# One more turn for the FFN: merged weights of a row made in the following turn, with a new timetable

## The reference, cut to what matters

```
h   = layernorm(x)
q   = (h @ Wq.T + bq) / sqrt(16);  k = ctx @ Wk.T + bk;  v = ctx @ Wv.T + bv      # 16 heads
a   = softmax(q @ k.T, over keys) @ v
y   = x + (a @ Wo.T + bo)
g   = layernorm(y)
out = y + ((g @ W1[r].T + b1[r]) @ W2[r].T + b2[r])      # row r has its own W1 (1024x256), W2 (256x1024)
```

## Time and profile before

| what | us |
|---|---|
| median of three runs | 609.21 (607.52 to 611.81) |
| the profiled execution | 607.91 |
| its span, first to last instruction | 606.1 |
| busy: PE, DVE, ACT, POOL | 563.9, 457.4, 392.5, 273.5 |
| TensorE's granted clock, mean | 0.966 |

### The profile page before, as it was taken

How to read it: one execution, slowest core, us unless ns; L and a number is a source line. 1 busy time by engine, 2 the same in 40 slices (tenths; PEclk the granted TensorE clock), 3 DMA queues, 4 the chain that set the end, 5 groups by cost and what they waited for, 6 DMA issues and landing times.

```text
span 606.1 us, 13508 instructions
## 1 busy us (share of the span) xinstructions
PE 563.9 (93%) x4353; PEld 342.9 (57%) x4353; DVE 457.4 (75%) x841; ACT 392.5 (65%) x703; POOL 273.5 (45%) x319
## 2 busy tenths in 40 slices
PE   7799999999999999999999999999899989898987
PEld 7545546565665656555655656565555646353667
DVE  6897896889678876888778876888778976883024
ACT  4225776777667676767767676777768665766541
POOL 5260466046832496046832487046831193017311
PEclk9957999999999999999999999999999999995999
DMA  6684343565444733464344723465434523420201
GB/s 208 130 221 158 87 112 84 134 194 132 105 115 118 227 85 94 136 185 135 105 99 130 226 76 100 119 184 152 105 90 106 159 49 96 129 84 6 86 0 36
DMA packets 46704, 72.67 MB, mean 120 GB/s; under 512 B 12162, under 2 KB 22730, under 8 KB 46666
## 3 DMA queue, kind: packets, MB, share of 16 engines
q1 hardware_dynamic: 46666, 72.18, 43.0%
HBM read 41.99 MB, written 4.47 MB: 77 GB/s over the span
## 4 chain that ended last, share of the span: by engine, by line
PE 65%; DVE 16%; issue 9%; ACT 5%; POOL 2%; DMA 2%; DVEq 1%; SPq 0%; ACTq 0%; POOLq 0%
PE pv L535 16%; PE st L521 13%; PE nat L510 10%; PE misc L709 9%; PE misc L595 7%; DVE neg_max L1040 5%; PE misc L585 3%; DVE stats L1051 3%; ACT probs L878 2%; DVE lo L1062 2%; ACT normed L926 2%; DVE y L1119 2%; POOL norm_in L1277 1%; PE st L501 1%; DVE normedT_lo L1068 1%
## 5 line engine op out<-in xcount | busy, mean ns | idle before, releaser
L1040 DVE TENSOR_REDUCE neg_max<-nat 128x1 f32<-128x512 f32 x504 | 336.9, 683 | 99.3 <-PE nat L510 94.9
L878 ACT ACTIVATE probs<-st 128x512 f32<-128x512 f32 x502 | 293.1, 599 | 147.3 <-PE st L521 136.0
L521 PE MATMUL st<-qs,ks 64*128 64x512 f32 x502 | 229.0, 472 | 14.9 <-ACT probs L878 14.3
L510 PE MATMUL nat<-ks,qs 63*128 63x512 f32 x504 | 236.0, 488 | 5.1 <-DVE neg_max L1040 2.4
L521 PEld LDWEIGHTS st<-qs,ks 64*128 64x128 f32 x502 | 92.9, 190 | 127.9 <-ACT probs L878 114.8
L535 PE MATMUL pv<-probs,vs 128*32 128x512 f32 x1024 | 140.2, 620 | 1.2 <-ACT probs L878 1.2
L510 PEld LDWEIGHTS nat<-ks,qs 63*128 63x128 f32 x504 | 92.8, 189 | 32.0 <-DVE neg_max L1040 26.7
L709 PE MATMUL misc<-w_in 64*128 64x256 f32 x512 | 70.7, 378 | 8.3 <-DVE y L1128 8.3
L709 PEld LDWEIGHTS misc<-w_in 64*128 64x128 f32 x512 | 51.4, 186 | 16.0 <-issue 11.0
L1298 POOL TENSOR_TENSOR pair_ctx<-pair_ctx,inv_sum 128x512 f32<-128x512 f32 x15 | 19.1, 1271 | 89.0 <-DMA inv_sum<-inv_dram 89.0
L535 PEld LDWEIGHTS pv<-probs,vs 128*32 128x32 f32 x1024 | 20.3, 108 | 37.4 <-issue 27.9
(11 more groups left out here) (204 smaller groups left out, 1005.9 us busy)
## 6 DMA issues: line engine op xcount, KB each, us to landing
ks<-hi SPq DMA_DIRECT2D x64, 128.0 KB, 2.4
qs<-hi SPq DMA_DIRECT2D x64, 128.0 KB, 2.5
w_in<-w SPq DMA_DIRECT2D x16, 512.0 KB
w_in<-w2T SPq DMA_DIRECT2D x16, 512.0 KB
x_in<-x SPq DMA_DIRECT2D x8, 512.0 KB, 3.4
ctx_in<-ctxT SPq DMA_DIRECT2D x8, 512.0 KB, 3.6
ks<-lo SPq DMA_DIRECT2D x32, 128.0 KB, 2.4
qs<-lo SPq DMA_DIRECT2D x32, 128.0 KB, 2.5
```

Of the source, the lines that this page charges most:

```text
L510: mm((nat_of(n) if bank is None else bank)[:, :], qs[own, 2 * g + jj, c * P:(c + 1) * P], ks[own, 2 * g + jj, :], start=True, stop=True).t ...
L521: mm(st_of(u, prep)[:, :], ks[rows(jp), 2 * g + jj, kc * P:(kc + 1) * P], qs[rows(jp), 2 * g + jj, :], start=True, stop=True).then_inc(st_ ...
L878: act.activation(probs[kc % 2][:, j, :], st_of(u, prep)[:, :], ACT.Exp).then_inc(exp_done, 1)
L1040: dve.tensor_reduce(neg_max[:, g % 2, at:at + 1], (nat_of(n) if bank is None else bank)[:, :], AX.X, ALU.max, negate=True).then_inc(max_do ...
```

## The change

- W21 of row b is made in turn b + 1 (units 33 to 47) between the last chain links, its split follows at units 47 to 49, `yT` moves to units 51 and 52, and `z` to units 55 to 64, so its last step lies in unit 0 of the turn after. The output halves are added on VectorE in units 1 and 3 of turn b + 2 (`late` is true where there is a row b - 2).
- Turn 0 makes no W21. Turn 7 makes that of row 6 at units 10 to 15 and that of row 7 at units 51 to 63, with tables of its own.
- The FFN load of row b stands at the end of turn b on SP, the one of row 0 no longer before the turns. `store_out` and `load_y` move into the first third of the next turns, `spread_ln` behind `gather_sums`, and `spread_inverse(b, 0)` behind `stack_quad(b + 1, 1)`.
- POOL makes the b2 parts of row b - 1 first in turn b, then `divide` and `add_bo`; `inverse_root(1)` stands ahead of `x_norm`, `add_b2` behind the stacks of v.
- The tables have new units throughout, and `yT`, `z`, `W21` and `maxT` other banks.

The diff, cut to its core:

```diff
-YT_BANKS = (1, 2)
-Z_BANKS = (1, 2)
-W21_BANKS = (0, 1)
-MAXT_BANKS = (2, 1, 2, 0)
-
-CHAIN_UNITS = tuple((4 * k + 2, 4 * k + 2, 4 * k + 3, 4 * k + 3, 4 * k + 4, 4 * k + 4) for k in range(LINKS + 1))
-YT_UNITS = (38, 38, 38, 38, 39, 39, 39, 39)
-Z_UNITS = (44, 44, 45, 45, 47, 47, 48, 49)
-W21_UNITS = (51, 52, 52, 54, 54, 55, 56, 56, 58, 59, 60, 60, 62, 62, 63, 63)
-LAST_W21_UNITS = (50, 50, 51, 51, 52, 52, 54, 54, 55, 56, 56, 58, 58, 59, 60, 60)
-MAXT_UNITS = ((54, 55), (6, 7), (23, 24), (39, 40))
+YT_BANKS = (0, 2)
+Z_BANKS = (1, 0)
+W21_BANKS = (1, 2)
+MAXT_BANKS = (1, 1, 2, 0)
+
+CHAIN_UNITS = ((3, 3, 3, 3, 3, 5), (7, 7, 7, 7, 7, 8), (10, 10, 11, 11, 12, 12), (14, 15, 15, 15, 15, 16), (18, 18, 19, 19, 19, 20), (22, 22, 22, 23, 24, 24), (27, 27, 27, 27, 27, 27), (31, 31, 31, 31, 31, 32), (33, 33, 33, 34, 35, 36))
+YT_UNITS = (51, 51, 51, 51, 52, 52, 52, 52)
+Z_UNITS = (55, 56, 59, 59, 60, 63, 63, 64)
+W21_UNITS = (33, 35, 36, 38, 38, 38, 39, 39, 42, 42, 43, 44, 45, 46, 47, 47)
+LAST_W21_UNITS = (51, 51, 51, 51, 51, 51, 51, 51, 53, 54, 56, 59, 60, 60, 62, 63)
+EARLY_W21_UNITS = (10, 10, 10, 11, 11, 11, 11, 13, 15, 15, 15, 15, 15, 15, 15, 15)
+LAST_YT_UNITS = (39, 40, 42, 42, 43, 43, 43, 43)
+LAST_Z_UNITS = (48, 48, 48, 48, 48, 48, 48, 48)
+MAXT_UNITS = ((52, 53), (4, 5), (23, 24), (37, 39))
 PV_AT = 1
 
-ODD_AT = (34, 2)
-JOIN_AT = (36, 4)
+ODD_AT = (33, 1)
+JOIN_AT = (43, 5)
 EVEN_AT = (19, 51)
-MASK_AT = (22, 54)
-HI_AT = (9, 13, 17, 21)
-LO_AT = (10, 14, 18, 22)
-W21_HI_AT = 0
-W21_LO_AT = 2
-ATTN_AT = (50, 16)
-NORM_AT = 33
-YT_HI_AT = 40
-YT_LO_AT = 41
-X_SPLIT_AT = 52
-CTX_SPLIT_AT = 44
-STATS_AT = 11
-INVERT_AT = (40, 7)
-MAX_AT = (56, 8, 25, 41)
-Y_AT = (25, 29)
-V_AT = (33, 37)
-OUT_AT = (50, 51)
+MASK_AT = (20, 61)
+HI_AT = (8, 12, 16, 20)
+LO_AT = (9, 13, 19, 21)
+W21_HI_AT = (47, 48, 49)
+W21_LO_AT = (48, 49)
+ATTN_AT = (60, 15)
+NORM_AT = 36
+YT_HI_AT = (52, 53)
+YT_LO_AT = (52, 53)
+X_SPLIT_AT = 44
+CTX_SPLIT_AT = 41
+STATS_AT = 15
+INVERT_AT = (37, 7)
+MAX_AT = (53, 7, 24, 39)
+Y_AT = (25, 31)
+V_AT = (31, 36)
+OUT_AT = (65, 67)
+
+EARLY_W21_HI_AT = (17, 18, 20)
+EARLY_W21_LO_AT = (19, 21)
+LAST_YT_HI_AT = (43, 44)
+LAST_YT_LO_AT = (44, 45)
+LAST_OUT_AT = (49, 63)
+LAST_W21_BANKS = (0, 1)
...
-            def turn(b, post, prep, load):
-                if post:
-                    stack_quad(b, 3)
-                    gather_sums(b - 1, 1)
+            def turn(b, late, post, prep, load):
                 if load:
                     load_x(b + 2)
+                if late:
+                    store_out(b - 2, 0)
                 if post:
+                    gather_sums(b - 1, 1)
+                    stack_quad(b, 3)
                     save_inverse(b - 1, 1)
                 store_max(b, 1)
                 if post:
                     spread_inverse(b - 1, 1)
-                if load:
-                    load_xT(b + 2)
+                if late:
+                    store_out(b - 2, 1)
+                if post:
+                    load_y(b - 1)
                 if prep:
                     stack_quad(b + 1, 0)
+                store_max(b, 2)
                 if load:
                     save_ln(b + 2)
-                    spread_ln(b + 2)
-                if post:
+                    load_xT(b + 2)
+                if not prep:
                     load_ffn(b, 0)
-                store_max(b, 2)
-                if post:
                     load_ffn(b, 1)
                     load_bias(b)
+                if load:
+                    load_ctx(b + 2)
+                gather_sums(b, 0)
+                if load:
+                    spread_ln(b + 2)
+                save_inverse(b, 0)
+                store_max(b, 3)
                 if prep:
                     stack_quad(b + 1, 1)
-                gather_sums(b, 0)
-                if load:
-                    load_ctx(b + 2)
-                save_inverse(b, 0)
-                store_max(b, 3)
                 spread_inverse(b, 0)
+                if not prep:
+                    store_out(b - 1, 0)
                 if prep:
                     stack_quad(b + 1, 2)
-                if post:
-                    store_out(b - 1, 0)
+                    load_ffn(b, 0)
+                    store_max(b + 1, 0)
+                    load_ffn(b, 1)
+                    load_bias(b)
+                if not prep:
                     store_out(b - 1, 1)
-                if prep:
-                    store_max(b + 1, 0)
-                load_y(b)
+                    load_y(b)
...
-            load_ffn(0, 0)
-            load_ffn(0, 1)
-            load_bias(0)
...
                 if prep:
                     if k == 0:
                         wait(pe, ctx_ready, b + 2)
-                        wait(pe, max_ready, 4 * b + 1)
+                        if late:
+                            wait(pe, yT_ready, 2 * (b - 1))
                     if k == 1:
                         wait(pe, xT_ready, b + 1)
-                        wait(pe, w21_ready, b)
-                        wait(pe, b2_ready, b)
+                        if late:
+                            wait(pe, out_ready, 2 * (b - 1))
                     if k == 2:
                         wait(pe, max_ready, 4 * b + 2)
                     if k in (3, 4, 5):
...
+                        if late:
+                            wait(pe, out_ready, 2 * (b - 1))
+                    if k == 5 and not prep:
                         wait(pe, w21_ready, b)
                         wait(pe, b2_ready, b)
-                    if k == 5:
-                        wait(pe, max_ready, 4 * b + 2)
...
-            def w21_begin(b, post, prep):
+            def w21_begin(b, prep):
                 wait(pe, ffn_loaded, 96 * (b + 1))
-                wait(pe, max_ready, 4 * b + 4)
                 if prep:
-                    wait(pe, lo_ready, 4 * (b + 1) + 3)
-                    wait(pe, v_ready, 2 * (b + 1) + 2)
-                if post:
-                    wait(pe, out_ready, 2 * b - 1)
-
-
-            def jobs(b, u, post, prep):
-                for n, at in enumerate(W21_UNITS):
-                    if post and at == UNITS + u:
-                        w21_step(b - 1, n, True)
+                    wait(pe, y_ready, 2 * b + 2)
+                    wait(pe, v_ready, 2 * (b + 2) + 1)
+                else:
+                    wait(pe, max_ready, 4 * (b + 1) + 2)
+
+            def last_w21_begin():
+                wait(pe, ffn_loaded, 96 * B)
+                wait(pe, out_ready, 2 * LAST)
+
+            def yT_begin(b, prep):
...
+            def z_begin(b, prep):
+                wait(pe, yT_ready, 2 * b + 2)
+                wait(pe, w21_ready, b + 1)
+                if prep:
+                    wait(pe, max_ready, 4 * (b + 2) + 1)
+                else:
+                    wait(pe, y_ready, 2 * b + 2)
...
+            def jobs(b, u, late, post, prep):
+                for n, at in enumerate(Z_UNITS):
+                    if late and at == UNITS + u:
+                        if n == 0:
+                            z_begin(b - 2, True)
+                        z_step(b - 2, n)
                 for t, at in enumerate(MAXT_UNITS[1]):
...
+                for n, at in enumerate(EARLY_W21_UNITS):
+                    if not prep and at == u:
+                        if n == 0:
+                            w21_begin(b - 1, prep)
+                        w21_step(b - 1, n, W21_BANKS, True)
...
-                            wait_apart(pe, norm_ready[1], 4 * b)
-                        yT_step(b - 1, n)
+                            w21_begin(b - 1, prep)
+                        w21_step(b - 1, n, W21_BANKS, True)
...
+                for n, at in enumerate(Z_UNITS if prep else LAST_Z_UNITS):
+                    if post and at == u:
+                        if n == 0:
+                            z_begin(b - 1, prep)
+                        z_step(b - 1, n)
+                for n, at in enumerate(LAST_W21_UNITS):
+                    if not prep and at == u:
+                        if n == 0:
+                            last_w21_begin()
+                        w21_step(b, n, LAST_W21_BANKS, False)
...
-                        if u == W21_HI_AT:
+                        w21_at = W21_HI_AT if prep else EARLY_W21_HI_AT
+                        if u == w21_at[0]:
                             w21_copy(b - 1, 0)
-                        if u == W21_HI_AT + 1:
+                        if u == w21_at[1]:
                             b2_copy(b - 1)
-                        if u == W21_HI_AT + 2:
+                        if u == w21_at[2]:
                             w21_copy(b - 1, 1)
...
                     for row, n in nats_of(b, u, post, prep):
                         row_max(row, n)
-
+                    if late and u + UNITS in OUT_AT:
...
-            def turn(b, post, prep, load):
+            def turn(b, late, post, prep, load):
                 if post:
                     v_stack(b, 3)
```

(29 more changed lines are left out.)

121 lines of the change are left out of this document (66 added, 55 removed).

## The result

The changed kernel takes **582.39 us** (median of 4 runs, 581.48 to 591.07) against 610.51 for the kernel before beside it (607.52 to 613.15): ratio **0.954, 95% interval 0.947 to 0.960**. The prediction said 600.5, range 589 to 612. The profiled execution took 581.72 us, its span 579.9, so 1.8 lie outside, as before.

What follows compares the result with a forecast made beforehand. No single engine bounds it: each short stretch takes its busiest engine's time, plus waits at jobs' first steps. Turn 0 -3.9, turns 1 to 6 -7.8, turn 7 +4.3 sum to -7.4: 600.5 us, range 589 to 612.

Steps and rivals of the forecast that it cites:

- Turns 1 to 6: Steady turns: old waits go, new ones come, net -1.3 us a turn, -7.8 us over six turns.
- the three waits: Steady turns: W21's first step 1.3 us, normalise 0.8, maxT of group 2 0.4; all go, -2.5 us a turn.
- The new waits: Steady turns: z at unit 55 comes 0.8 us late, W21's copies wait 0.4 us at unit 47.
- VectorE as co-bound: Steady turns: row maxima take 64 x 0.683 = 43.7 us of VectorE, tied to TensorE and ScalarE within two units.
- Turn 0: Units 49 to 63 without W21, at 0.84 us a unit: -3.9 us, bounds 7.3 and 2.0.
- Turn 7: Last turn: row 6's W21 +4.0 us, clock rising four units later +1.1, normalise's wait -0.8; together +4.3.
- Covers: Transfers and queued POOL work have spare time, divide 2 us, invert at unit 7 about 1 us; all counted at nothing.
- Tail: After the last turn: row 7's y wants b2 parts and add_bo only some 8 us after the last exponential; nothing.
- The port: Rival, 0.02: VectorE joins wait out POOL instructions, up to 0.72 us, +4.3 us over six turns: 604.8 us.
- Moved, not removed: Second rival, 0.20: turns 1 to 6 keep 68.5 us, VectorE as full as before; +0.4 us, 608.3 us.
- More than counted: First rival, 0.18: no new waits in turns 1 to 6, dense units 10 to 15 keep turn 7's clock up: 588.8 us.

Runs made afterwards that it cites:

- chain alone: Kernel before with the changed kernel's chain units, high and low parts, y_half, statistics and normalise, W21 left at the turn's end: 617.97 us, ratio 1.010.
- chain, split at 56: Kernel of chain alone with ScalarE's split of the attention's first half at unit 56 in place of 50: 606.04 us, ratio 0.989.
- change with old chain: Changed kernel with the chain and its neighbours in the units of the kernel before, W21 still mid-turn: 598.14 us, ratio 0.977.
- F: Changed kernel with the SP order of C, VectorE's reciprocal at unit 6 and ScalarE's second-half attention split at unit 16: 571.2 us, ratio 0.936.
- the kernel with four early steps: Changed kernel with only 4 of 16 W21 steps of row 6 in units 10 to 15 of turn 7: 580.82 us, ratio 0.952.
- C: Changed kernel with SP's order recast: ks pieces of quad 3 ahead of the save, qs pieces behind the spread: 580.9 us, ratio 0.951.
- D: Changed kernel with the SP order of C and VectorE's reciprocal of the second pair one unit earlier, at unit 6: 572.6 us, ratio 0.938.
- E: Changed kernel with the SP order of C and ScalarE's split of the second attention half at unit 16, not 15: 573.8 us, ratio 0.943.

## Why the prediction was wrong

Quarters of turn 4 in us (the row with * is turn 3, which has 3.4 us at 1.2 GHz in its third quarter), for the argument:

| kernel | first | second | third | last | turn |
|---|---|---|---|---|---|
| before | 15.2 | 17.1 | 17.7 | 18.5 | 68.5 |
| chain alone | 15.2 | 15.5 | 17.5 | 21.5 | 69.8 |
| chain, split at 56 * | 15.2 | 15.4 | 18.8 | 18.5 | 67.9 |
| change with old chain | 17.3 | 15.3 | 19.4 | 14.3 | 66.4 |
| changed | 17.0 | 14.7 | 18.0 | 14.3 | 64.0 |
| F | 14.7 | 15.3 | 18.0 | 14.3 | 62.3 |

- **Turns 1 to 6** are the step that failed: -7.8 forecast, -22.5 measured. It took "the three waits" (-2.5) as all that goes. Shown: W21's 1.3 us, with the 0.9 of the split's wait, were worth 0.2 us in the old timetable, and `normalise`'s 0.8 left its stretch at 5.5; what goes is idle time of TensorE spread over third and last quarter (2.85 to 0.52 us in turn 4, 3.56 to 0.58 with four W21 steps of 16) and 1.6 of the second quarter's 2.4 us in products draining alone, which the three named waits don't list. Turn 4 of four kernels, all at full clock: the split FFN way with the old chain gives 2.1 us, the chain with a later split 0.2, both together 4.5. Over the whole time they give 2.3%, 1.1% and 4.6%: the two are worth more together than apart. My own estimate said it: a need of 59 us against 68.5. I had used the 9.5 us between them only for a rival of 0.18, and capped even that at the named waits.
- **The new waits** that it named were sized well. z was to wait 0.8: turn 3 shows 0.7 for the low part (at the weight load) and 0.4 for the copy of the maxima. W21's copies were to wait 0.4 at unit 47: 0.7. W21's first step waits for nothing, as said.
- **VectorE as co-bound** was sized by durations, 64 x 0.683. Back to back, maxima start 0.61 apart (two take 1.29 us from start to end, one 0.68), so 64 of them need 39 us of a turn, not 43.7. That made "as full as before", in the second rival, look like a bound.
- **Turn 0**: -3.9 forecast, -4.2 measured: the step by units without W21 held. The 1.6 us that the profiled execution lost ahead of turn 0 are in no term.
- **Turn 7**: +4.3 forecast, -2.5 measured. W21's part held: +4.0 for 16 steps, and 12 of them cost 3.2 us (3.5 over the whole turn). (The first quarter grew by 5.7, 13.65 to 19.35; the rest of that is there with four steps too.) The clock failed: it was to be at 1.2 GHz until unit 48 and stayed at 2.4; the third quarter went from 21.3 to 14.1 us. The reason given by the first rival, the dense units 10 to 15, is refuted by the kernel with four early steps. In F the clock falls for 3.4 us near unit 40 and the quarter takes 15.5 (mean clock 0.89); in the kernel before with four W21 steps of 16, mean clock 0.90, 17.8. So some 2.3 us of it come at nearly equal clock, beside six of z's eight steps, which went from this quarter to unit 48; about 5, by this estimate, are the clock. C, D and E have 6.8, 10.2 and 6.8 us at 1.2 GHz in turn 7, the two traces of the changed kernel none. What decides it was not found, so the miss by the clock is a fact and its cause stays open.
- **Covers.** `divide` was given 2 us of cover behind the b2 parts. The parts were indeed no wait (POOL was free 2.04 us before), but the spread, which stands on SP behind stack, save and maxima, was, with 2.8 us on ScalarE. I had checked POOL's queue and not SP's for that transfer. `invert` at unit 7 held, with a unit to spare: at unit 6 (D) it paid.
- **Tail**: 0 forecast, +1.5 measured, with the clock at 1.2 GHz for 3.4 us at 557.9 where it had been up before.
- **The port**: counted at nothing, and wrong: it holds VectorE for 0.27 us in a steady turn (last section). What that is worth in time was not measured.
- **Rivals.** "Moved, not removed" is refuted. "More than counted" had the sign and most of the size (588.8), partly by luck: one event was right (the clock of turn 7 stays up) for a wrong reason, and the turns were again capped at the named waits.

## What to carry over

A named wait is worth its length only if TensorE (or whichever engine bounds) idles in it and has slack in the units right behind; read the window of the wait and the next one together: at unit 50 the next was full and the gain was 0.2 of 2.2 us, at unit 15 it was not and the gain was all of TensorE's 2.0 us. Where an engine's need by starts (not durations) is far below the turn, forecast from that gap and ask what a looser timetable could take of it, rather than add up the waits that the trace names. Look for one part of a change that only pays with another: here the new chain gained nothing until ScalarE no longer waited for the division.
